# Part of the second phase of a two-phase kernel is run inside the first, in slots of four channels by 32 batches

## The reference, cut to what matters

```python
x = x + einsum('bct,bcd->bdt', x, weights[condition])        # u, what follows reads it
K = 2*real(einsum('hn,hnl->hl', Ct, exp(dtA[:, :, None]*arange(2048))))
y = irfft(rfft(u, 4096) * rfft(K, 4096)[None])[..., :2048]   # causal convolution, per channel
y = (y + u*D[:, None]) * (arange(2048)[None, :] < length[:, None])[:, None, :]
return u + y
```

## Time and profile before

| | |
|---|---|
| median of the runs | 1072.36 us |
| the profiled execution: span, first to last instruction | 1073.5 us |
| mixing, to the end of the last batch's matmuls | 312.4 us |
| from there to the second slot's `inputs_to_state` | 22.4 us |
| 62 slots from there | 718.7 us, 11.59 us each |
| from the last `inputs_to_state` to the end | 20.1 us |

### The profile page before, as it was taken

How to read it: one execution, slowest core, us unless ns; L and a number is a source line. 1 busy time by engine, 2 the same in 40 slices (tenths; PEclk the granted TensorE clock), 3 DMA queues, 4 the chain that set the end, 5 groups by cost and what they waited for, 6 DMA issues and landing times.

```text
span 1073.5 us, 30051 instructions
## 1 busy us (share of the span) xinstructions
PE 1004.2 (94%) x11612; PEld 741.1 (69%) x11612; DVE 717.1 (67%) x1647; ACT 580.4 (54%) x1230; POOL 654.8 (61%) x1377
## 2 busy tenths in 40 slices
PE   7977779778999999999999999999999999999998
PEld 4333234233347887888888888888888888888886
DVE  3988950000006877788788788778778778888875
ACT  2643444344535555566566556556655656656654
POOL 3211051201207887888888888888888888888740
PEclk9999999899999999999999999999999999999999
DMA  8999999999989999999999999999999999999994
GB/s 323 424 421 424 423 422 423 363 424 424 424 314 326 292 281 261 252 230 229 232 225 234 223 233 235 224 234 222 230 224 225 226 212 250 224 223 229 237 220 124
DMA packets 169630, 305.01 MB, mean 284 GB/s; under 512 B 78274, under 2 KB 111426, under 8 KB 161298
## 3 DMA queue, kind: packets, MB, share of 16 engines
q1 hardware_dynamic: 169170, 302.64, 98.5%
q0 software_dynamic: 160, 0.20, 0.1%
q10 hardware_dynamic: 160, 0.26, 0.1%
HBM read 152.37 MB, written 134.41 MB: 267 GB/s over the span
## 4 chain that ended last, share of the span: by engine, by line
PE 77%; DMA 17%; ACT 3%; issue 2%; DVE 0%; SPq 0%; ACTq 0%
PE bank L603 16%; DMA u_scratch<-stage 15%; PE bank L617 15%; PE bank L570 14%; PE bank L556 11%; PE bank L544 9%; PE bank L582 7%; PE bank L609 5%; ACT stage L743 2%; DMA x_f<-in_x 1%; DMA gt_sb<-g_sb 0%; ACT ring L743 0%; DMA u_row<-u_scratch 0%; DMA u_scratch<-ring 0%; DVE st_sb L1039 0%
## 5 line engine op out<-in xcount | busy, mean ns | idle before, releaser
L603 PE MATMUL bank<-toep,u_t 128*128 128x192 f16 (+1 forms) x3072 | 342.5, 220 | 0.2
L617 PE MATMUL bank<-g_sb,st_sb 128*128 128x256 f16 x1536 | 306.0, 273 | 0.8 <-issue 0.8
L544 PE MATMUL bank<-x_f,w_buf 128*128 128x512 f32 x512 | 243.0, 621 | 52.1 <-ACT stage L743 29.0
L556 PE MATMUL bank<-ident,u_row 128*128 128x128 f32 x1024 | 277.5, 275 | 4.4 <-DMA u_row<-u_scratch 1.7
L773 ACT ACTIVATE st_sb<-bank 128x128 f16<-128x128 f32 x448 | 123.8, 276 | 256.3 <-PE bank L582 194.1
L603 PEld LDWEIGHTS bank<-toep,u_t 128*128 128x128 f16 x3072 | 231.4, 99 | 13.7
L544 PEld LDWEIGHTS bank<-x_f,w_buf 128*128 128x128 f32 x512 | 95.9, 196 | 190.3 <-issue 116.7
L1057 DVE COPY_PREDICATED o_sb<-mask,u_row 128x512 f32<-128x512 uint8 x256 | 212.5, 830 | 16.6 <-issue 16.5
L1034 DVE SCALAR_TENSOR_TENSOR u_t<-bank,u_t 128x512 f16<-128x512 f32 x256 | 176.1, 688 | 56.0 <-ACT u_t L757 56.0
L1039 DVE TENSOR_TENSOR st_sb<-bank,st_sb 128x128 f16<-128x128 f32 x448 | 130.4, 291 | 88.3 <-ACT st_sb L773 83.2
L609 PE MATMUL bank<-toep,x_t 128*128 128x64 f16 x2048 | 188.2, 193 | 0.2 <-issue 0.2
(11 more groups left out here) (135 smaller groups left out, 969.5 us busy)
## 6 DMA issues: line engine op xcount, KB each, us to landing
x_f<-in_x SPq DMA_DIRECT2D x64, 1024.0 KB, 19.6
u_row<-u_scratch SPq DMA_DIRECT2D x128, 512.0 KB, 5.9
out<-o_sb SPq DMA_DIRECT2D x254, 256.0 KB, 3.8
u_scratch<-stage SPq DMA_DIRECT2D x48, 1024.0 KB, 17.7
toep<-k_scratch SPq DMA_DIRECT2D x64, 256.0 KB, 6.1
u_scratch<-ring SPq DMA_DIRECT2D x14, 512.0 KB, 14.6
u_scratch<-kept SPq DMA_DIRECT2D x12, 448.0 KB, 6.5
gt_sb<-g_sb SPq DMA_TRANSPOSE x124, 5.4
```

What stands on the lines that cost most here:

```text
L544: last = pe.matmul(bank[:, 4 * (n % 2) + k, :], w_buf[n % XS][:, :], x_f[n % XS][:, k * 512:(k + 1) * 512], start=True, stop=True)
L556: last = pe.transpose(bank[:, 4 + q, g * P:(g + 1) * P], u_row[c % 4][:, h, g, tb * P:(tb + 1) * P], ident[:, :])
L603: pe.matmul(bank[:, y, col + tb * P + NM:col + Q], u[:, h, tb, a, rows_], t[:, h, b, NM:Q - tb * P], start=first, stop=False, skip_group_c ...
L617: last = pe.matmul(bank[:, y, col:col + Q], st[:, h, a, gr * ROWS:(gr + 1) * ROWS], g[:, h, b, :], start=False, stop=(m == 2), skip_group_ ...
```

## The change

The two phases overlap. The slots are of two kinds now, both of 512 columns for each of PE's banks:

- a **wide** slot has four channels and 32 batches. The first 48 channels are done so, in 12 wide slots of the first 32 batches (part 0) and 12 of the last 32 (part 1);
- a **full** slot has two channels and 64 batches, as before. The other 80 channels are done so, in 40 slots.

Slots 0 to 11 are wide, part 0. Then one wide slot of part 1 follows every third full slot. There are 64 slots, as before. 35 batches are mixed as before. Batch 35 is mixed between the transposes of slot 0, and the last 28 within slots 0 to 9, two or three to a slot, by quarters of 512 steps in banks 6 and 7, of which ACT empties one and DVE the other. While this lasts, u is transposed through banks 4 and 5 alone; the last 32 batches have three x buffers (six before), and there are eight half stages for the first 32 batches and four for the others.

A wide slot has the tables of two pairs of channels, so two Toeplitz loads and two pairs of DMA transposes. POOL makes g once; it is stored to `g_dram` in part 0 and loaded in part 1. DVE makes `lam` for the first 12 slots. Each half batch is stored with two DMAs (48 channels in pieces of 2 KB into `u_wide`, 80 in pieces of 4 KB into `u_full`). The tables of slots 0 and 1 now come by DMA transposes, where PE turned them before; the filler matmuls (`work`) ahead of and in slot 0 are gone, and so are the kept halves.

```diff
+WIDE = 12
+FIRST = 35
+XS, WS, STAGES = 6, 6, 8
+MIXED = [3, 3, 3, 3, 2, 3, 3, 3, 2, 3]
+QUARTERS = {2: (1, 1, 1, 1, 1, 1, 1, 1), 3: (2, 1, 2, 1, 2, 1, 2, 1)}
...
+SLOTS = [Slot(True, 4 * i, 0, True) for i in range(WIDE)]
+for i in range(H // 2 - 2 * WIDE):
+    SLOTS.append(Slot(False, H1 + 2 * i, 0, True))
+    if i % 3 == 2 and i // 3 < WIDE:
+        SLOTS.append(Slot(True, 4 * (i // 3), 1, False))
...
+X_AT = [n % XS if n < NBW else n % (XS // 2) for n in range(NB)]
+STAGE_AT = [m % STAGES if m < 2 * NBW else m % (STAGES // 2) for m in range(2 * NB)]
...
 # SP
+                if n == FIRST - 2:
+                    transpose_g(0)
+                if n == FIRST - 1:
+                    stages_landed(sp, range(STAGES), NBW)
+                    sp.wait_ge(s_masks, 1)
+                    for h in range(4):
+                        load_u(0, h)
...
+            def mixing_slot(c):
+                for k in range(8):
+                    if k == 0:
+                        if c > 0:
+                            load_toeplitz(c)
+                        if has(c - 2):
+                            store_out(c - 2, 3)
+                        load_u(c + 1, 3)
+                    if k == 3:
...
+                        transpose_g(c + 1)
+                    if k in (3, 5, 7):
+                        if has(c - 1):
+                            store_out(c - 1, k // 2 - 1)
+                        load_u(c + 2, k // 2 - 1)
+                    for n, q in MIX_AT[c][k]:
+                        if q % 2 == 1:
+                            store_half(n, q // 2)
+                        if q == 3 and n + 3 < NB:
+                            load_x(n + 3)
...
 # PE
+            def mix(n, k):
...
+                if k % 2 == 0:
+                    pe.wait_ge(s_ev, 2 * n + k // 2)
+                else:
+                    wait(pe, s_evd, 2 * i + k // 2)
+                pe.matmul(bank[:, 6 + k % 2, :], w_buf[n % WS][:, :], x_f[X_AT[n]][:, k * 512:(k + 1) * 512],
+                          start=True, stop=True).then_inc(s_mq, 1)
...
+                for h in range(channels(s)):
+                    t, hh = tab(s, h)
                     for m, (a, b) in enumerate(SPLIT):
+                        last = pe.matmul(ap(bank, h * NJ * width(s) + at(s, j), [[1, width(s)]]),
+                                         lam_sb[t % LS][:, hh, a, :, :].rearrange("p k m -> p (k m)"),
...
+                    if has(c - 1):
+                        taps_part(c - 1, k, between)
+                        states_part(c - 1, k, between)
...
+                    for n, q in MIX_AT[c][k]:
+                        mix(n, q)
+                    if has(c) and k >= 2:
+                        advance(c, k - 1)
```

More of the change, by code:

```diff
@@ L61, in ap, with before, uses, u_bank @@
+def before(places, i):
+    last = [j for j in range(i) if places[j] == places[i]]
+    return last[-1] if last else None
+def uses(places, i):
+    return places[:i].count(places[i])
+def u_bank(s, q):
+    return 4 + (q % 2 if s <= LATER else q)
+def u_bank_before(s, q):
+    for r, p in ((r, p) for r in range(s, -1, -1) for p in range(3, -1, -1)):
+        if (r, p) < (s, q) and u_bank(r, p) == u_bank(s, q):
+            return r, p
+    return None
 def ap(t, offset, dims, parts=P, first=0):
@@ L235, in split_halves, with slots, has @@
-        def split_halves(n):
-            return [1] if n < HELD_FROM else [0] if n < BOTH_FROM else [0, 1]
+        def slots(body):
+            for c in range(NSL + 2):
+                body(c)
+        def has(c):
+            return 0 <= c < NSL
         def wait(eng, s, value):
-            if not isinstance(value, int) or value > 0:
+            if value > 0:
                 eng.wait_ge(s, value)
-        def at(j):
-            return (j % NG * JJ + j // NG) * NB
-        def state(t, part, j):
-            return ap(t, part * NG * ROWS + at(j), [[2 * NG * ROWS, 2], [1, NB]])
@@ new lines, in x_at, with tab, lam_by_dve, backward @@
+        def x_at(s, h, tb, g):
+            if SLOTS[s].wide:
+                return UNIT * h + 2 * P * tb + P * g
+            return UNIT * (2 * h + tb) + P * g
+        def tab(s, h):
+            return TABS[s][h // 2], h % 2
+        def lam_by_dve(s):
+            return s < WIDE
+        def backward(half):
+            return half.rearrange("p (b t) -> p b t", t=P)[:, :, ::-1]
+        def backward_to(half):
+            return half.rearrange("p (b t) -> p b t", t=P)
+        def loads_of_g(t):
+            return sum(not SLOTS[SLOT_OF[r]].made for r in range(t % GS, t + 1, GS))
@@ new lines, in load_u @@
+            def load_u(s, h):
+                b, last = ROW_AT[s], before(ROW_AT, s)
+                if SLOTS[s].wide:
+                    if last is not None:
+                        sp.wait_ge(s_ov, 4 * last + h + 1)
+                    src = bass.AP(u_wide, ((SLOTS[s].first + h) * 2 + SLOTS[s].part) * (P * UNIT), [[UNIT, P], [1, UNIT]])
+                    sp.dma_start(u_row[b][:, UNIT * h:UNIT * (h + 1)], src).then_inc(s_row[b][h], 16)
+                else:
+                    if last is not None:
+                        sp.wait_ge(s_ov, 4 * last + 2 * h + 2)
+                    src = bass.AP(u_full, (SLOTS[s].first - H1 + h) * (P * HALF), [[HALF, P], [1, HALF]])
+                    sp.dma_start(u_row[b][:, HALF * h:HALF * (h + 1)], src).then_inc(s_row[b][h], 16)
@@ new lines, in transpose_u @@
+            def transpose_u(s, k):
+                q = k // 4
+                if SLOTS[s].wide:
+                    h, tb, g = q, k // 2 % 2, k % 2
+                else:
+                    h, tb, g = q // 2, q % 2, k % 4
+                b = ROW_AT[s]
+                if k % (16 // channels(s)) == 0:
+                    loads = sum(ROW_AT[r] == b and channels(r) > h for r in range(s + 1))
+                    pe.wait_ge(s_row[b][h], 16 * loads)
+                if k % 4 == 0:
+                    last = u_bank_before(s, q)
+                    if last is not None:
+                        pe.wait_ge(s_ul, 4 * last[0] + last[1] + 1)
+                    elif u_bank(s, q) >= 6:
+                        pe.wait_ge(s_ev, 2 * NB)
+                        pe.wait_ge(s_evd, 2 * (NB - FIRST))
+                ins = pe.transpose(bank[:, u_bank(s, q), k % 4 * P:(k % 4 + 1) * P],
+                                   ap(u_row[b], (h * groups(s) + g) * Q + tb * P, [[1, P]]), ident[:, :])
+                if k % 4 == 3:
+                    ins.then_inc(s_ut, 1)
@@ L683, in _ @@
+            slots(slot)
         @block.scalar
@@ L816, in _ @@
-            slots(act, slot)
+                            fold_toeplitz(of)
+                        elif SLOTS[of].made:
+                            for t in TABS[of]:
+                                g_hi(t)
+            slots(slot)
             for v in range(2):
```

968 lines of the change are left out of this document (499 added, 469 removed).

## The result

The changed kernel takes **1272.12 us**, the median of four runs (1265.78 to 1273.84), against 1072.23 us for the kernel before (1071.67 to 1075.35). The ratio is 1.185, with a 95% interval of 1.182 to 1.188. The forecast was 1101 us with a range of 1056 to 1136: the sign was right, the size wrong by a factor of seven (+200 us in place of +29). The profiled execution is the shortest of the four (1265.78 us), with a span of 1263.5 us.

A forecast was written before the change was run, and what follows sets the result against it. Mixing was taken as bound by the DMA engines, the second phase by PE. The sum 203 + 254 + 624.8 + 20.1 = 1101.9 us of span gave 1101 us against 1072.4, slower by 2.7%, range 1056 to 1136.

The forecast's parts named there:

- The ten mixing slots: Slots 0 to 9 with 28 batches: DMA-bound, 194 us of traffic at 424 GB/s plus 60 us of tables, 254 us.
- neither becomes the bound: In the 53 slots after, SP (13.6 us of issues a wide slot) and DMA (12.2 us) were not to bind.
- PE's price of a wide slot: PE work in a wide slot: +0.75 us (0 to 1.1) over a full slot's 11.59, so 12.34 us.
- 624.8 us for 53 slots: From slot 10 to slot 63: 14 wide slots at 12.34 us and 39 full ones at 11.59 (613 to 630).
- The tables: DMA cost in the mixing slots: 2.0 us for transposes plus 1.0 for Toeplitz loads a pair, 60 us in all.
- The start: Time to the first `inputs_to_state`, after batches 0 to 31 are stored and u is loaded back: 203 us (197 to 210).
- The 35 batches before keep their pace: Mixing ahead of the first slot was to run as before, with the store of batch 31 issued at 165.3 us.
- Rival 1: Mixing slots: the tables' traffic is hidden and PE sets them, 223 us, total 1070 us; chance 0.26.
- Rival 2: Mixing slots: SP's order binds, 29.5 us a slot, ten of them +31 us, total 1132 us; chance 0.12.
- Rival 3: Mixing slots: the overlap fails as u or x landings are late, 1121 us and up to 1150; chance 0.06.
- The prize: PE's idle time an overlap can win: 29 us in the last 29 batches, and some of 22.3 between the phases.

The follow-up runs named there:

- 128 rows: Changed kernel with each wide slot's output stored as one store of 128 rows of 2 KB into a scratch area, those outputs left out: 1169.93 us, ratio 1.087.
- and no transposes: Changed kernel with wide outputs stored over 128 scratch rows, and the DMA transposes of slots 1 to 9 left out: 1128.18 us, ratio 1.048.
- experiment 7: Here: changed kernel, wide outputs stored over 128 scratch rows, the u loads of slot 0 issued ahead of the first transposes: 1181.27 us, ratio 1.092.
- experiment 3: Changed kernel with 57 batches mixed before the first slot and only six in slots 0 and 1: 1282.76 us, ratio 1.186.
- experiment 1: Changed kernel with the mixing slots' stage stores issued by ACT instead of SP: 1279.79 us; with the x loads there on ACT too: 1317.70 us.

## Why the prediction was wrong

**The step that failed** stood under "The ten mixing slots": "for each slot 2.10 MB of u and outputs ... 194 us at 424 GB/s". Half of these bytes, the outputs, move on four engines: the mixing slots had 260 GB/s, and took 347.5 us in place of 254. I took a rate from a phase in which the large transfers had 64 or more rows outermost and laid it on one whose pattern I had not read for its outermost dimension, though the diff shows it. The same step carried "neither becomes the bound" for the slots after. With the pattern spread, everything else equal, the spans divide so:

| stretch, us | forecast | changed | 128 rows | and no transposes |
|---|---|---|---|---|
| to the first `inputs_to_state` | 203 | 229.4 | 228.2 | 229.9 |
| slots 0 to 9 | 254 | 347.5 | 288.5 | 244.8 |
| 53 slots | 624.8 | 666.6 | 630.9 | 630.9 |
| end | 20.1 | 20.0 | 20.1 | 20.3 |
| span | 1101.9 | 1263.5 | 1167.7 | 1125.9 |

The four engines cost some 95 of the 162 us by which the span was missed: 59 in the mixing slots and 36 in the others.

**PE's price of a wide slot: right.** The prediction took 0.30 us for the twelve small matmuls of an advance. PE in time in the changed kernel:

```profile
233.59 0.46 PE L781 MATMUL bank<-st_wide,lam_sb 128*128 128x32 f16 x12
233.89 0.42 PE L747 MATMUL bank<-ident,u_row 128*128 128x128 f32 x2
```

From the first of them to the next group are 0.30 us. Where nothing disturbs them wide slots take 12.1 us, full ones 11.3 to 11.5, so both are some 0.2 us under what I took, and their difference is 0.6 to 0.8 (0.75 taken). The forecast's 624.8 us for 53 slots met 630.9 with the spread store, 5.6 of the 6 being slot 10, still behind.

**The tables: roughly right.** Their transposes cost 2.3 us a pair (2.0 taken) in two pairs of runs, 2.8 in the first pair if the chip's own level is taken out by the ratio. The 1.0 us for the Toeplitz loads was tried by no run.

**The start: 26 us late, and only told in part.** "The 35 batches before keep their pace" was wrong: batch 32 is mixed at 176.4 us and not at 164.3, and the windows at 40 and 120 us move 348 and 398 GB/s. The kernel before, in the same stretches:

```profile
40.00:80.00 40.00, 32.91 (x70) 13.08 (x68) 36.66 (x97) 19.78 (x22) 5.00 (x9) 0.96 1.02 422
120.00:150.00 30.00, 22.43 (x64) 9.03 (x65) 26.39 (x68) 11.63 (x12) 5.40 (x14) 1.00 1.02 423
```

From 30 to 165 us SP's issues sum to 129 us, where the kernel before had 67: four stores a batch in place of one. The four stores of batch 31 are issued at 181.7 to 185.6 us, 16 to 20 later than the 165.3 that I took from the earlier trace rows. Here is PE in time at the start, then SP's queue:

```profile
176.43 3.70 PE L713 MATMUL bank<-x_f,w_buf 128*128 128x512 f32 x8
...
190.00 9.85 PE L713 MATMUL bank<-x_f,w_buf 128*128 128x512 f32 x16 [9.76 <-DMA x_f<-in_x]
217.00 1.94 PE L747 MATMUL bank<-ident,u_row 128*128 128x128 f32 x8 [17.16 <-DMA u_row<-u_wide]
218.74 5.63 PE L726 MATMUL bank<-x_f,w_buf 128*128 128x512 f32 x8
```

```profile
181.66 1.04 SPq L385 DMA_DIRECT2D u_wide<-stage  x1
...
185.58 0.57 SPq L387 DMA_DIRECT2D u_full<-stage  x1
...
189.72 6.95 SPq L435 DMA_TRANSPOSE gt_sb<-g_sb  x2
196.72 0.58 SPq L439 DMA_DIRECT2D g_scratch<-g_sb  x1
197.48 6.69 SPq L435 DMA_TRANSPOSE gt_sb<-g_sb  x2
204.22 0.58 SPq L439 DMA_DIRECT2D g_scratch<-g_sb  x1
...
209.00 3.04 SPq L395 DMA_DIRECT2D u_row<-u_wide  x4
```

PE waits 9.76 us for x: batch 33 goes into the buffer of batch 30, as the last 32 batches have three buffers, and its load is issued only at 181.1 us. It waits 17.16 us for u, whose loads I had at 183 us and which are issued at 209.0. The transposes of the first two pairs, which I had left out of the start, hold SP for 14 of the 26 us between. From the landing of u to the first `inputs_to_state` PE takes 12.4 us and not the 6.5 that I took, since four transposes of slot 1 and six records of batch 36 stand there too. Issuing u of slot 0 ahead of the tables did not help (experiment 7). Batch 35 runs partly at the lower level of 1.2 GHz (mean granted clock 0.69 in this stretch, after the waits): 5.63 us, where eight such records take 3.70 at 2.4 GHz.

**The 34.5 us that remain in the mixing slots** are not settled. The sum had the engines at 424 GB/s between the transposes. Without transposes they are at 348. The four engines are excluded as the cause. Taking the stage stores off SP gained nothing, but that test put waits of 13 us on the splits in their place, so a part of SP's queue is not excluded. PE's lower granted clock (0.89, 0.96 without transposes) goes with its waits, and whether it adds to them was not tried.

**The rivals.** Rival 1 (PE sets the slots) did not come: PE is busy 72% of the mixing slots. Rival 2 (SP's order) was the likeliest reading of the trace, and most of its price did not come when its issues were taken away (22.7 us of issues a slot were forecast and over 32 seen, but they stayed at the same sum with some 100 fewer). Rival 3 (landings) named a wait that is there, for u rather than x, but its reason was wrong: in experiment 3 it is there in wide slots without mixing (31.8 us from 420 to 565 us). The prize was a little smaller than I said, too: the earlier trace rows has PE busy 113.35 of the 135.5 us, so 22 us idle and not 29. The mechanism that decided was none of the three.

## What to carry to other kernels

Before a rate is taken for a new transfer, read its access pattern from the outside: an outermost dimension of 4 cost 246 us in a kernel whose bytes, issues and matmuls were unchanged, 8 cost 41, 16 nothing. In a profile short windows at a share of a quarter say that few engines work; a mean share near 1 beside a low rate does not, since the kernel before has 0.99 at 229 GB/s with all in order. The waits that show up are those of other transfers. And test "the queue is full" by taking issues away: if the issues that stay grow longer and the sum stays the same, part of their length was waiting. Then look at what the engine that took the issues over now delays.

## What the runs showed of the hardware

- A window in which four or five packets are under way moves 90 GB/s at a share of 0.27 (experiment 3, 507.5 to 510.5 us).
- Four stores of 64 KB in place of one of 256 KB, all with 32 or more rows outermost, cost 0.19 us of the kernel's time for each one added.
- Issues on SP do not have one length: two transposes of the same shape took 6.95 us at 189.7 us, in full traffic, and 2.54 us in the earlier trace rows; in experiment 1 a load of u went from 1.08 to 2.33 us.
- In the first mixing phase, four stores of 192 and 320 KB a batch went with 348 to 398 GB/s, where one store of 1 MB had 422, with the same number of buffers for x and for stages. Whether smaller transfers, SP's longer list of issues or, in the first of the two stretches, the ten small loads of the lengths at 59 to 67 us (two before) make the difference was not tried.
